# Two heads' scores in one block: the order of work in the wide attention stage is rewritten by pairs of heads

## The chip, the cores and the metric

The kernel runs on one core of one Trainium2 chip. The metric is the device time of one launch in microseconds. Three timed runs of the kernel before gave 1787.20, 1788.65 and 1789.53 us, median 1788.65 us. All float32 operands stay float32 to the outside; large products are made of three matmuls on a high part and a low rest of each operand.

## The reference, cut to what matters

The program is a sequence of transformer layers on x of 32 x 64 tokens by 256. The change lies in the first two layers, two cross-attentions to the same context with 16 heads of 128 and one learned key and value beside the 64 tokens of the context:

```python
H, K = 16, 128
qh = (q_in @ wq + bq).reshape(b, q_len, H, K)
kh = (kv_in @ wk + bk).reshape(b, t, H, K)
vh = (kv_in @ wv + bv).reshape(b, t, H, K)
kh = jnp.concatenate([kh, jnp.broadcast_to(bias_k, (b, 1, H, K))], axis=1)
vh = jnp.concatenate([vh, jnp.broadcast_to(bias_v, (b, 1, H, K))], axis=1)
logits = jnp.einsum('bqhk,bthk->bhqt', qh, kh) / scale
weights = jax.nn.softmax(logits, axis=-1)
ctx = jnp.einsum('bhqt,bthk->bqhk', weights, vh).reshape(b, q_len, H * K)
return ctx @ wo + bo
```

Ahead of each is a layer norm of x, behind it x is added back. An MLP and further layers follow and are not touched.

## The kernel before, in words

`wide_attentions` (L91 to L805) does both cross-attentions in one stream. The 2048 tokens form NG = 4 groups of 512 (GT = 4 tiles of 128). A pass takes HP = 2 heads; there are PASSES = 8 passes for each of the two attentions, so 16 passes of four groups, 64 pairs of heads and group. Within a pass the items are (group, head), ITEMS = 8 of them, and `passes` (L215) calls `slots(i, j, ...)` once for each on every engine. Each engine has its own copy of the stream in its own fixed order (POOL L341, PE L415, ACT L574, DVE L714); semaphores tie them together, and no planner is involved.

The slot of an item on TensorE (PE) has this order: turn the weights of the item before it (two transposes, L437); project its own queries (6 matmuls of 512 columns, through `product`, L81 to L83); attend for the item before it (L457, 8 instructions of 128 columns); project its keys (6 of 512); project half of the values of the pair (12 of 256); in the second head's slot, the output projection of the pair before (24 of 256, into o_ps); last its own scores (L504, 16 instructions of 65 columns on 64-column halves of the array). So the scores of one head end a slot, and the weights made from them are turned at the start of the slot after the next.

ScalarE (ACT) copies each result out of PSUM: the turned weights (L582, two halves), queries (L597), attended values (L600), the exponentials (L603), keys (L606), values (L618). VectorE (DVE) makes the softmax: maximum (L721), difference (L726), sum (L745), reciprocal (L747), weights (L749), besides the low rest of the attended values (L742) and the addition to x (L776, two heads together, which frees o_ps). GpSimd (POOL) makes low parts of the weight matrices (L322, L359), copies head biases (L317, L318) and, where a norm is due, the normalised rows (L338) and the low part of h (L348).

Some slots carry more work. TURNS turns the normalised rows of a group (8 transposes, L406) after the scores of the slot; VALUES makes the rows of the learned values (L535); the last pass of an attention (`ending_group`) adds one transpose (L441) and four products (L494) to each pair. In a slot of two heads' pair the old order puts a full slot, some 6 to 9 us, between the scores and the transposes of their weights.

## Time and profile before

| what | value |
|---|---|
| median of three runs | 1788.65 us |
| the profiled execution's own time | 1789.56 us |
| its span, first to last instruction | 1787.8 us |
| TensorE busy over the span | 1689.2 us (94%) |
| ScalarE, VectorE, GpSimd busy | 995.4, 940.1, 549.9 us |
| mean granted TensorE clock | 0.975 |
| wide stage: first and last addition to x (L776) | 48.4 and 1029.7 us |

The profiled execution lies 0.91 us above the median. Times of rows are counted from the start of its span. The wide stage takes the first 1031 us; everything behind it is the same in both kernels. "Busy" of TensorE is modelled from the starts of its instructions, so distances between starts say more than durations.

### The profile page before, as it was taken

What the parts mean: (1) busy time and instruction counts of PE and PEld (TensorE: products, weight loads), DVE (VectorE), ACT (ScalarE), POOL (GpSimd) and SP (SyncE); (2) the same over time, 40 slices, a digit from 0 to 9 for tenths busy, and PEclk for the clock granted to TensorE, in tenths of its full rate; (3) what the DMA queues carried; (4) which work ended last, traced back from release to release, by engine and by line L of the source; (5) the groups of instructions that cost most, each with busy time, mean ns of one, the idle gap of its engine ahead of it and who ended that gap; (6) DMA issues with size and microseconds to landing.
All of it is one profiled execution on the core that took longest, in us unless ns stands there. A gap on an engine that the chain in (4) does not pass through costs nothing. (4 is left out here: it accounts for less than half of the span.)

```text
span 1787.8 us, 36048 instructions
## 1 busy us (share of the span) xinstructions
PE 1689.2 (94%) x14356; PEld 1445.4 (81%) x14356; DVE 940.1 (53%) x2064; ACT 995.4 (56%) x1932; POOL 549.9 (31%) x601
## 2 busy tenths in 40 slices
PE   7999999999999999999999889899989799987699
PEld 6999999999889899999998778676766567765598
DVE  6644444444455444444444364477859656667432
ACT  4545555555545455555555355467648667776444
POOL 5301000100153010001001162257744478776311
PEclk9999999999999999999999899899989999999699
DMA  6030000000000000000000010300010000001001
GB/s 191 1 121 24 0 23 23 23 0 24 25 1 25 25 9 15 23 23 2 21 23 0 1 31 1 86 20 2 2 22 1 7 1 2 2 13 31 1 12 36
DMA packets 59135, 40.02 MB, mean 22 GB/s; under 512 B 15725, under 2 KB 58263, under 8 KB 59031
## 3 DMA queue, kind: packets, MB, share of 16 engines
q1 hardware_dynamic: 57414, 37.78, 7.4%
q8 instruction: 73, 1.20, 0.3%
q10 hardware_dynamic: 1616, 0.79, 0.2%
q14 instruction: 32, 0.25, 0.0%
HBM read 36.46 MB, written 2.10 MB: 22 GB/s over the span
## 5 line engine op out<-in xcount | busy, mean ns | idle before, releaser
L582 ACT ACTIVATE l0a_weight_t<-l0a_t_ps 64x256 f32<-64x256 f32 x256 | 97.0, 379 | 266.3 <-PE l0a_t_ps L437 256.6
L742 DVE TENSOR_TENSOR l0a_c_lo<-l0a_c_ps,l0a_c_hi 128x512 fp32r<-128x512 f32 x128 | 88.5, 692 | 236.7 <-ACT l0a_c_hi L600 236.7
L776 DVE TENSOR_TENSOR x<-l0a_o_ps,x 128x1024 f32<-128x1024 f32 x64 | 78.4, 1225 | 213.2 <-PE l0a_o_ps L83 174.8
L317 POOL COPY l0a_head_bias<-l0a_bias_cols 128x2 f32 (+1 forms) x32 | 6.3, 198 | 494.8 <-DVE l0a_logit L726 491.0
L81 PE MATMUL l0a_o_ps<-l0a_wo_hi,l0a_c_hi 128*128 128x256 f32 x512 | 149.6, 292 | 1.5 <-ACT l0a_c_hi L600 1.5
L457 PEld LDWEIGHTS l0a_c_ps<-l0a_weight_t,l0a_v 128*128 128x128 f32 x1024 | 133.9, 192 | 13.9 <-ACT l0a_weights_t L585 2.7
L82 PE MATMUL l0a_o_ps<-l0a_wo_lo,l0a_c_hi 128*128 128x256 f32 x512 | 144.6, 282 | 0.0
L83 PE MATMUL l0a_o_ps<-l0a_wo_hi,l0a_c_lo 128*128 128x256 f32 x512 | 144.6, 282 | 0.0
L81 PE MATMUL l0a_v_ps<-l0a_wv_hi,ctx_hi 128*128 128x256 f32 x512 | 144.3, 282 | 0.0
L82 PE MATMUL l0a_v_ps<-l0a_wv_lo,ctx_hi 128*128 128x256 f32 x512 | 144.2, 282 | 0.0
L83 PE MATMUL l0a_v_ps<-l0a_wv_hi,ctx_lo 128*128 128x256 f32 x512 | 142.9, 279 | 0.0
L457 PE MATMUL l0a_c_ps<-l0a_weight_t,l0a_v 128*128 128x128 f32 x1024 | 135.9, 276 | 2.0 <-ACT l0a_weights_t L585 1.1
L606 ACT ACTIVATE l0a_k<-l0a_k_ps,l0a_head_bias 128x512 f32<-128x512 f32 x128 | 88.3, 690 | 60.4 <-PE l0a_k_ps L83 60.2
L597 ACT ACTIVATE l0a_q<-l0a_q_ps,l0a_head_bias 128x512 f32<-128x512 f32 x128 | 88.1, 688 | 58.4 <-PE l0a_q_ps L83 57.6
L618 ACT ACTIVATE l0a_v<-l0a_v_ps 128x512 f32<-128x512 f32 x128 | 76.6, 598 | 76.3 <-PE l0a_v_ps L83 76.3
L81 PE MATMUL l0a_q_ps<-h_hi,l0a_w_hi 128*128 128x512 f32 x256 | 112.3, 439 | 0.7 <-POOL l0a_k L318 0.7
L81 PE MATMUL l0a_k_ps<-ctx_hi,l0a_w_hi 128*128 128x512 f32 x256 | 112.1, 438 | 0.0
L82 PE MATMUL l0a_k_ps<-ctx_lo,l0a_w_hi 128*128 128x512 f32 x256 | 101.4, 396 | 0.0
L83 PE MATMUL l0a_q_ps<-h_hi,l0a_w_lo 128*128 128x512 f32 x256 | 101.3, 396 | 0.0
L81 PEld LDWEIGHTS l0a_v_ps<-l0a_wv_hi,ctx_hi 128*128 128x128 f32 x512 | 96.2, 188 | 6.2
L82 PE MATMUL l0a_q_ps<-h_lo,l0a_w_hi 128*128 128x512 f32 x256 | 101.0, 394 | 0.0
L83 PE MATMUL l0a_k_ps<-ctx_hi,l0a_w_lo 128*128 128x512 f32 x256 | 100.7, 394 | 0.0
(435 smaller groups left out, 4883.2 us busy)
## 6 DMA issues: line engine op xcount, KB each, us to landing
l0a_raw_v<-in_L_xattn_wv_dram SPq DMA_DIRECT2D x16, 256.0 KB, 3.3
l0a_raw_o<-in_L_xattn_wo_dram SPq DMA_DIRECT2D x32, 128.0 KB, 2.8
l3a_room<-in_L_xattn_wo_dram SPq DMA_DIRECT2D x2, 2048.0 KB, 8.7
l0a_raw<-in_L_xattn_wq_dram SPq DMA_DIRECT2D x31, 128.0 KB, 2.3
l0a_raw<-in_L_xattn_wk_dram SPq DMA_DIRECT2D x31, 128.0 KB, 2.3
x<-in_x_dram SPq DMA_DIRECT2D x4, 512.0 KB, 8.0
l3a_room<-in_L_xattn_w_fc_dram SPq DMA_DIRECT2D x2, 1024.0 KB, 11.2
l3a_room<-in_ctx_dram SPq DMA_DIRECT2D x1, 2048.0 KB, 11.1
```

What stands on the lines that cost most here:

```text
L81: pe.matmul(out, wh, mh, start=start, stop=False)
L82: pe.matmul(out, wh, ml, start=False, stop=False)
L83: return pe.matmul(out, wl, mh, start=False, stop=stop)
L317: pool.tensor_copy(head_bias[p][:], bias_cols[:, BQ:BK + 1, bass.ds(h, 1)].rearrange("p a b -> p (a b)"))
L457: last = pe.matmul(by_tile[:, m, b, :, :], v[(j - HP) // HP % 2][:, m * HB + b, p * K:(p + 1) * K], weight_t[:, m, b, :, :].rearrange("p a ...
L582: last = act.activation(weight_t[half, :, :, b, :], t_ps[half, 0:GT // 2 * P] .rearrange("p (m b q) -> p m b q", b=HB, q=SEQ), ACT.Copy)
L597: act.activation(q[:], q_ps[:], ACT.Identity, bias=head_bias[p][:, 0:1]).then_inc(q_done, 1)
L606: act.activation(k[p][:, :, 0:SEQ], k_ps[:].rearrange("p (b k) -> p b k", k=SEQ), ACT.Identity, bias=head_bias[p][:, 1:2]).then_inc(k_done, 1)
L618: act.activation(v[j // HP % 2][:, p * GT // HP:(p + 1) * GT // HP, :] .rearrange("p t k -> p (t k)"), v_ps[:], ACT.Copy).then_inc(v_done, 1)
L742: dve.tensor_tensor(c[p][1][:], c_ps[:], c[p][0][:].bitcast(F32), ALU.subtract).then_inc(c_lo, 1)
L776: dve.tensor_tensor(chip.x[:, own, :], o_ps[:], chip.x[:, own, :], ALU.add).then_inc(added, 1)
```

## The change

The slot now belongs to a pair of heads and a group: `slots(i, u, ...)` with u from 1 to 4 replaces eight slots of single heads, on all engines.

On TensorE the order of a slot is: queries and keys of the first head; (rows turned, learned values, where due); the first half of the values; the four transposes of the weights of both heads of the pair before; queries of the second head; the second half of the values; attend for the first and for the second head of the pair before; keys of the second head; the output projection of the pair before; the scores of both heads of this pair, 32 instructions in one block.

The scores of the two heads lie in two PSUM banks (s_ps, 2 x 512), and the softmax is done once for both: the maximum, the difference, the exponential, the sum, the reciprocal and the weights each work on twice the elements with one instruction. To find the banks, the keys and the turned weights share one (kt_ps), and the second head's attended values are written into the queries' bank (q_ps). On ScalarE the exponential stands behind the taking of the first head's queries and ahead of its keys; the two heads' turned weights are copied in four pieces. Queries have one SBUF tile for each head. Head biases of the next pass are copied by GpSimd at the start of the next pass's first slot, behind the scores (L317, L318), and ScalarE waits for them before it takes the queries. The rows of a group are turned between the keys and the values of a slot instead of after its scores; in slot 0, ahead of the second head's keys.

```diff
-    TURNS = {0: 1, 2: 2, 4: 3, **{(PASSES - 1) * ITEMS + 6 + HP * g: NG + g for g in range(NG)}, LAST * ITEMS + 6: 2 * NG}
-    VALUES = {ITEMS: 0, (PASSES + 1) * ITEMS: 1}
-    SPREAD = {HP * HP: 0, ITEMS + 1: 1}
+    TURNS = {0: 1, 1: 2, 2: 3, **{(PASSES - 1) * NG + 3 + g: NG + g for g in range(NG)}, LAST * NG + 3: 2 * NG}
+    VALUES = {NG: 0, (PASSES + 1) * NG: 1}
+    SPREAD = {2: 0, NG: 1}
...
-        q, k = sb("q", [P, GN]), [sb(f"k{p}", [P, GT * HB, SEQ + 1]) for p in range(HP)]
+        q, k = [sb(f"q{p}", [P, GN]) for p in range(HP)], [sb(f"k{p}", [P, GT * HB, SEQ + 1]) for p in range(HP)]
         v = [sb(f"v{b}", [P, GT, HP * K]) for b in range(2)]
-        logit, expd = sb("logit", [P, GT, SEQ + 1]), sb("expd", [P, GT, SEQ + 1])
-        top, total, inverse = sb("top", [P, GT]), sb("total", [P, GT]), sb("inverse", [P, GT])
...
-        weight_t = sb("weight_t", [P, GT // 2, HB, 2, SEQ])
+        HT = HP * GT
+        logit, expd = sb("logit", [P, HT, SEQ + 1]), sb("expd", [P, HT, SEQ + 1])
+        top, total, inverse = sb("top", [P, HT]), sb("total", [P, HT]), sb("inverse", [P, HT])
...
-        q_ps, k_ps, v_ps, s_ps, t_ps, c_ps = (chip.ps(f"l0a_{x}_ps", [P, GN], stack) for x in ("q", "k", "v", "s", "t", "c"))
+        q_ps, kt_ps, v_ps, c_ps = (chip.ps(f"l0a_{x}_ps", [P, GN], stack) for x in ("q", "kt", "v", "c"))
+        s_ps = chip.ps("l0a_s_ps", [P, HP, 512], stack)
...
+        attended = (c_ps, q_ps)
...
+                def slots(i, u, this, prev, a=0):
...
+                    if this and u == NG:
+                        pool.wait_ge(s_made, n)
+                        for p in range(HP):
+                            last = head_columns((i + 1) * HP + p, p)
+                        last.then_inc(head_set, 1)
...
+                    if next_pass_in(i, u):
+                        pool.wait_ge(w_hi_done, (i + 1) * HP + 1)
+                        low_w(0).then_inc(w_split, 1)
                     if S is not None and S + 1 in TURNS:
                         normalise(TURNS[S + 1])
...
+                    if next_pass_in(i, u):
+                        pool.wait_ge(w_hi_done, (i + 1) * HP + HP)
+                        low_w(1).then_inc(w_split, 1)
...
+                    def attend(p):
+                        by_tile = attended[p][:].rearrange("p (m a b q) -> p m b a q", a=2, b=HB, q=SEQ)
+                        for m in range(GT // 2):
+                            for b in range(HB):
+                                last = pe.matmul(by_tile[:, m, b, :, :], v[(u - 1) % 2][:, m * HB + b, p * K:(p + 1) * K],
+                                                 weight_t[p][:, m, b, :, :].rearrange("p a q -> p (a q)"), start=True, stop=True)
+                        last.then_inc(c_made, 1)
...
+                        if u % NG == 0:
+                            pe.wait_ge(w_split, (i + u // NG) * HP + 1)
+                        if first_use(S) is not None and S > 0:
+                            pe.wait_ge(x_lo_done, CH * (first_use(S) + 1))
+                        project(0, 0)
+                        if S in (0, 2, 3):
+                            pe.wait_ge(ctx_lo_done, {0: 4, 2: 6, 3: 8}[S])
+                        project(1, 0)
+                    if S in TURNS and S > 0:
+                        if S == 1:
+                            pe.wait_ge(x_whole_done, CH * TURNS[S])
                         else:
                             pe.wait_ge(added, outputs_before(S))
...
+                        turn_rows(TURNS[S], half_banks)
...
+                    if this:
+                        if u % NG == 0:
+                            pe.wait_ge(wv_split, i + u // NG + 1)
+                        if prev:
+                            pe.wait_ge(v_done, heads_before(0))
+                        values(0)
...
+                    if prev:
+                        pe.wait_ge(weight_a, n)
+                        if this:
+                            pe.wait_ge(k_done, heads_before(1))
+                        for x in range(HT // 2):
+                            last = pe.transpose(kt_ps[:, x * P:(x + 1) * P], weight[:, 2 * x:2 * x + 2, :]
+                                                .rearrange("p t k -> p (t k)"), chip.ident[:])
+                        last.then_inc(t_made, 1)
+                        if ending is not None:
+                            pe.wait_ge(learned_done, n)
+                            pe.transpose(s_banks[0][:, 0:P], learned_weight[:, group_rows(ending), :]
+                                         .rearrange("p t w -> p (t w)"), chip.ident[:]).then_inc(learned_turned, 1)
...
+                        pe.wait_ge(q_done, heads_before(1))
+                        project(0, 1)
+                    if this:
+                        pe.wait_ge(v_done, heads_before(1))
+                        values(1)
+                    if S == 0:
+                        pe.wait_ge(cols_done, 1)
+                        turn_rows(TURNS[S], half_banks)
...
+                        pe.wait_ge(t_done, heads_before(-1))
+                        attend(0)
+                        pe.wait_ge(t_done, heads_before(0))
+                        if this:
+                            pe.wait_ge(q_done, heads_before(2))
+                        attend(1)
+                    if this:
+                        if S == 0:
+                            pe.wait_ge(k_done, 1)
+                        project(1, 1)
...
+                        for t in range(GT):
+                            tok = slice(t * P, (t + 1) * P)
+                            for x in range(HP):
+                                if t == 0:
+                                    pe.wait_ge(c_hi, heads_before(x - 1))
+                                    pe.wait_ge(c_lo, heads_before(x - 1))
+                                last = product(pe, o_ps[:, t, :], c[x][0][:, tok], c[x][1][:, tok],
+                                               wo[0][:, x, :], wo[1][:, x, :], start=x == 0, stop=x == HP - 1 and ending is None)
...
+                    if this:
+                        pe.wait_ge(q_done, heads_before(2))
+                        pe.wait_ge(k_done, heads_before(2))
+                        if prev:
+                            pe.wait_ge(shifted, n)
+                        for p in range(HP):
+                            for t in range(GT):
+                                for b in range(HB):
+                                    at = (t * HB + b) * SEQ
+                                    last = pe.matmul(s_ps[b * SEQ:(b + 1) * SEQ, p, t * (SEQ + 1):(t + 1) * (SEQ + 1)],
+                                                     q[p][:, at:at + SEQ], k[p][:, t // 2 * 4 + b * 2 + t % 2, :], start=True, stop=True)
+                        last.then_inc(s_made, 1)
+                    if S == 0:
+                        pe.wait_ge(ctx_lo_done, 5)
+                        turn_context(2, 1)
...
+                    if this:
+                        if u % NG == 0:
+                            act.wait_ge(head_set, i + u // NG + 1)
+                        take_queries(0)
                     if prev:
...
                         act.wait_ge(shifted, n)
                         act.activation(expd[:], logit[:], ACT.Exp, scale=SCALE).then_inc(exp_done, 1)
                     if this:
...
+                        take_keys(0)
...
+                    if this:
+                        take_values(0)
...
+                    if next_pass_in(i, u):
+                        split_w(i + 1, 0)
+                    if prev:
+                        act.wait_ge(t_made, n)
+                        for p in range(HP):
+                            for b in range(2):
+                                half = slice(b * SEQ, (b + 1) * SEQ)
+                                last = act.activation(weight_t[p][half, :, :, b, :], kt_ps[half, p * GT // 2 * P:(p + 1) * GT // 2 * P]
+                                                      .rearrange("p (m b q) -> p m b q", b=HB, q=SEQ), ACT.Copy)
+                            last.then_inc(t_done, 1)
...
                     if this:
...
+                        take_queries(1)
+                    if this:
+                        take_values(1)
+                    if S == 0:
+                        take_rows(TURNS[S], half_banks)
+                    if prev:
+                        for p in range(HP):
+                            act.wait_ge(c_made, heads_before(p - 1))
+                            act.activation(c[p][0][:], attended[p][:], ACT.Copy).then_inc(c_hi, 1)
+                    if this:
+                        take_keys(1)
+                    if next_pass_in(i, u):
+                        split_wv(i + 1)
+                        split_w(i + 1, 1)
...
+                    if prev:
...
                         dve.wait_ge(s_made, n)
...
+                        dve.tensor_reduce(top[:].rearrange("p (h t) -> p h t", h=HP), scored, AX, ALU.max).then_inc(top_done, 1)
...
+                        dve.tensor_tensor(by_head(logit[:]), scored, top[:].rearrange("p (h t a) -> p h t a", h=HP, a=1)
+                                          .to_broadcast([P, HP, GT, SEQ + 1]), ALU.subtract).then_inc(shifted, 1)
...
                         dve.wait_ge(exp_done, n)
                         dve.tensor_reduce(total[:], expd[:], AX, ALU.add).then_inc(total_done, 1)
                         dve.wait_ge(total_done, n)
                         dve.reciprocal(inverse[:], total[:]).then_inc(inverse_done, 1)
                         dve.wait_ge(inverse_done, n)
                         dve.tensor_tensor(weight[:], expd[:, :, 0:SEQ], inverse[:].rearrange("p (t a) -> p t a", a=1)
...
+                                          .to_broadcast([P, HT, SEQ]), ALU.mult).then_inc(weight_a, 1)
...
+                    if prev:
+                        for p in range(HP):
+                            dve.wait_ge(c_hi, i * (HP * NG) + HP * u + p - 1)
+                            dve.tensor_tensor(c[p][1][:], attended[p][:], c[p][0][:].bitcast(F32), ALU.subtract).then_inc(c_lo, 1)
...
+                    if prev:
+                        own = group_rows(u - 1)
```

## Rows read from the trace of the kernel before

**Rows 1.** One stretch: PE, PEld, DVE, ACT, POOL busy (count), clock, DMA share, GB/s.
```profile
200.00:300.00 100.00, 100.00 (x827) 90.37 (x826) 42.57 (x100) 52.39 (x101) 9.95 (x14) 1.00 0.07 21
```

**Rows 2.** Waits, 200 to 1100 us: who waited, for whom; total us, times, longest.
```profile
PE l0a_t_ps L437 <- DVE l0a_weight L749: 2.5, 1, 2.5
```

**Rows 3.** Timeline of TensorE, one pair of slots: start us, us, engine, line, operation, count.
```profile
303.88 0.44 PE L437 MATMUL l0a_t_ps<-ident,l0a_weight 128*128 128x128 f32 x2
...
304.39 0.39 PE L82 MATMUL l0a_q_ps<-h_lo,l0a_w_hi 128*128 128x512 f32 x1
...
305.32 0.39 PE L83 MATMUL l0a_q_ps<-h_hi,l0a_w_lo 128*128 128x512 f32 x1
305.55 1.05 PE L457 MATMUL l0a_c_ps<-l0a_weight_t,l0a_v 128*128 128x128 f32 x8
...
307.83 0.28 PE L81 MATMUL l0a_v_ps<-l0a_wv_hi,ctx_hi 128*128 128x256 f32 x1
...
309.25 0.28 PE L81 MATMUL l0a_o_ps<-l0a_wo_hi,l0a_c_hi 128*128 128x256 f32 x1
...
311.97 0.28 PE L83 MATMUL l0a_o_ps<-l0a_wo_hi,l0a_c_lo 128*128 128x256 f32 x1
312.18 0.69 PE L504 MATMUL l0a_s_ps<-l0a_k,l0a_q 128*64 128x65 f32 x16
312.80 0.44 PE L437 MATMUL l0a_t_ps<-ident,l0a_weight 128*128 128x128 f32 x2
...
318.88 0.44 PE L437 MATMUL l0a_t_ps<-ident,l0a_weight 128*128 128x128 f32 x2
```

**Rows 4.** Timeline of ScalarE in that slot.
```profile
305.75 0.69 ACT L597 ACTIVATE l0a_q<-l0a_q_ps,l0a_head_bias 128x512 f32<-128x512 f32 x1 [0.62 <-PE l0a_q_ps L83]
306.64 0.60 ACT L600 ACTIVATE l0a_c_hi<-l0a_c_ps 128x512 fp32r<-128x512 f32 x1 [0.20 <-PE l0a_c_ps L457]
307.13 0.41 ACT L603 ACTIVATE l0a_expd<-l0a_logit 128x260 f32<-128x260 f32 x1
```

**Rows 5.** Timeline of VectorE in that slot, and at the start of the next.
```profile
307.27 0.69 DVE L742 TENSOR_TENSOR l0a_c_lo<-l0a_c_ps,l0a_c_hi 128x512 fp32r<-128x512 f32 x1 [2.38 <-ACT l0a_c_hi L600]
307.88 0.41 DVE L745 TENSOR_REDUCE l0a_total<-l0a_expd 128x4 f32<-128x260 f32 x1
308.32 0.18 DVE L747 RECIPROCAL l0a_inverse<-l0a_total 128x4 f32<-128x4 f32 x1
308.54 0.42 DVE L749 TENSOR_TENSOR l0a_weight<-l0a_expd,l0a_inverse 128x256 f32<-128x256 f32 x1
...
312.29 1.22 DVE L776 TENSOR_TENSOR x<-l0a_o_ps,x 128x1024 f32<-128x1024 f32 x1 [3.25 <-PE l0a_o_ps L83]
313.43 0.42 DVE L721 TENSOR_REDUCE l0a_top<-l0a_s_ps 128x4 f32<-128x260 f32 x1
```

**Rows 6.** Groups by line and shape, 200 to 1100 us: busy us, mean ns, idle.
```profile
L504 PE MATMUL l0a_s_ps<-l0a_k,l0a_q 128*64 128x65 f32 x1680 | 72.0, 227 | 0.0
```

**Rows 7.** The same, 1100 to 1788 us, operations of other stages with 1024 elements.
```profile
L1766 DVE TENSOR_REDUCE l1a_top<-l1a_score 128x16 f32<-128x1024 f32 x32 | 38.9, 1215 | 0.6
L1713 ACT ACTIVATE l1a_score<-l1a_score 128x1024 f32<-128x1024 f32 x32 | 33.7, 1052 | 6.4 <-POOL l1a_score L1455 6.1
```

**Rows 8.** Timeline of TensorE: normalised rows turned in an ending slot.
```profile
1000.48 1.09 PE L406 MATMUL l0a_o_ps<-ident,l0a_rows 128*128 128x128 f32 x8
```

**Rows 9.** Timeline of GpSimd in the first slots.
```profile
32.40 4.85 POOL L338 TENSOR_SCALAR l0a_rows<-x,x_moments,l0a_norm_inverse 128x256 f32<-128x256 f32 x4
```

**Rows 10.** Timeline of TensorE where the wide stage runs out.
```profile
1012.12 0.44 PE L437 MATMUL l0a_t_ps<-ident,l0a_weight 128*128 128x128 f32 x2
...
1017.08 0.41 PE L437 MATMUL l0a_t_ps<-ident,l0a_weight 128*128 128x128 f32 x2 [2.51 <-DVE l0a_weight L749]
...
1018.75 2.08 PE L457 MATMUL l0a_c_ps<-l0a_weight_t,l0a_v 128*128 128x128 f32 x8 [1.15 <-ACT l0a_weights_t L585]
```

**Rows 11.** Timeline of VectorE there.
```profile
1016.51 0.42 DVE L749 TENSOR_TENSOR l0a_weight<-l0a_expd,l0a_inverse 128x256 f32<-128x256 f32 x1
```

More of the change, by code:

```diff
@@ L206, in next_head, with next_pass_in, ending_group @@
-        def next_head(i, j):
-            more = not (isinstance(i, int) and i == LAST)
-            return j - ITEMS + 1 if more and ITEMS - 1 <= j <= ITEMS else None
-        def ending_group(i, j):
-            return (j - HP) // HP if isinstance(i, int) and i in (PASSES - 1, LAST) and j % HP == HP - 1 else None
+            return S // NG // PASSES * NG + S % NG
+        def next_pass_in(i, u):
+            return u == NG - 1 and not (isinstance(i, int) and i == LAST)
+        def ending_group(i, u):
+            return u - 1 if isinstance(i, int) and i in (PASSES - 1, LAST) else None
@@ L215, in passes, with endings @@
+        def endings(i, u):
+            return i // PASSES * NG + u
         def passes(engine, slots):
-            slots(0, 0, True, False, False)
-            slots(0, 1, True, True, False)
-            for j in range(2, ITEMS + 2):
-                slots(0, j, True, True, True)
+            slots(0, 0, True, False)
+            for u in range(1, NG + 1):
+                slots(0, u, True, True)
             with engine.Fori(1, PASSES - 1) as i:
-                for j in range(2, ITEMS + 2):
-                    slots(i, j, True, True, True)
+                for u in range(1, NG + 1):
+                    slots(i, u, True, True)
@@ L233, in wide_attentions @@
+            for u in range(1, NG + 1):
+                slots(LAST, u, u < NG, True)
         with nc.Block() as block:
@@ L413, in turn_biases, with slots, heads_before, project @@
                     last.then_inc(cols_turned, 1)
-                def slots(i, j, this, mid, prev, a=0):
-                    n = i * ITEMS + j
-                    S = slot_number(i, j)
-                    p = j % HP
-                    _, cols = tiles(j)
-                    ending = ending_group(i, j)
-                    def project(x):
-                        out, made = ((q_ps, q_made), (k_ps, k_made))[x]
+                def slots(i, u, this, prev, a=0):
+                    n = i * NG + u
+                    S = slot_number(i, u)
+                    cols = group_columns(u % NG)
+                    ending = ending_group(i, u)
+                    def heads_before(more):
+                        return i * (HP * NG) + HP * u + more
+                    def project(x, p):
+                        out, made = ((q_ps, q_made), (kt_ps, k_made))[x]
                         src = ((chip.h_hi, chip.h_lo), (chip.ctx_hi, chip.ctx_lo))[x]
                         for ch in range(CH):
-                            if S == 0 and x == 0:
+                            if S == 0 and x == 0 and p == 0:
                                 pe.wait_ge(x_lo_done, ch + 1)
@@ new lines, in slots @@
+                    if prev:
+                        if S in (1, 2):
+                            pe.wait_ge(ctx_lo_done, {1: 7, 2: 8}[S])
+                        if not this:
+                            pe.wait_ge(v_done, heads_before(0))
+                        pe.wait_ge(t_done, heads_before(-1))
[4 more added lines that the diff above has]
+                        attend(1)
@@ L771, in slots @@
                         measure_group(m)
-                    if prev and p == HP - 1:
-                        own, _ = tiles(j - 2)
-                        dve.wait_ge(o_made, i * NG + (j - 1) // HP)
+                    if S in VALUES:
+                        keep_values(VALUES[S])
+                    if prev:
+                        for p in range(HP):
+                            dve.wait_ge(c_hi, i * (HP * NG) + HP * u + p - 1)
+                            dve.tensor_tensor(c[p][1][:], attended[p][:], c[p][0][:].bitcast(F32), ALU.subtract).then_inc(c_lo, 1)
+                    if next_pass_in(i, u):
+                        split_wv(i + 1)
+                    if S in SPREAD:
+                        spread_values(SPREAD[S])
+                    if S is not None and 1 <= S < 1 + NG:
+                        measure_context(S - 1)
+                    if prev:
+                        own = group_rows(u - 1)
+                        dve.wait_ge(o_made, n)
                         dve.tensor_tensor(chip.x[:, own, :], o_ps[:], chip.x[:, own, :], ALU.add).then_inc(added, 1)
```

315 lines of the change are left out of this document (107 added, 208 removed).

## The prediction

> **What bounds the kernel now.** I read the windows first. From 200 to 300 us TensorE is busy for 100.00 of 100 us at a granted clock of 1.00, with VectorE, ScalarE and GpSimd busy for 43, 52 and 10 [rows 1]. The reader is to see one full engine, so only a start that moves on TensorE moves the end. Busy time there is modelled, so I read the waits next: over 900 us TensorE waits once for the softmax weights before it turns them, 2.5 us, and that is where the stage runs out [rows 2, 10]. In the steady stretch nothing is late. Third, the timeline of a pair of slots, by distances between starts [rows 3]: 303.88 to 312.80 is 8.92 us, 312.80 to 318.88 is 6.08 us, together 15.00 us for a pair of heads and a group. There are 64 such pairs. The question is whether the new order gives TensorE less than 15.00 us of work and waiting.
>
> **TensorE's work by blocks** [rows 3]. Six products of 512 columns: (305.32 - 304.39) / 4 x 6 = 1.395 us. Turning one head's weights behind scores: 303.88 to 305.55 less the queries, 1.67 - 1.395 = 0.275. Attend for one head: 305.55 to 307.83 less the keys, 2.28 - 1.395 = 0.885. Half of the values: 309.25 - 307.83 = 1.42. Output projection, first to last start: 311.97 - 309.25 = 2.72. From the last product to the first score 0.21, where neighbours of this kind stand 0.12 apart; from the first score to the next operation 312.80 - 312.18 = 0.62. The 16 score instructions span 0.69 us with a last one of 0.23 [rows 3, 6], so 0.46 from first to last start and 0.16 from there to what follows.
>
> **What merging removes.** A score block costs about 0.09 more ahead of it and 0.13 more behind it than its own spacing, and its first steps are slow. The new slot has one block of 32 instead of two of 16. The instructions are as many as before; the second head's sixteen add about 0.48 to the first block. Transposes go from 2 + 2 to 4 in a row; one more costs (1.09 - 0.27) / 7 = 0.117, taking 0.27 as the length of one [rows 8]. So four cost 0.275 + 2 x 0.117 = 0.51.
>
> **What merging adds: the weights come later than TensorE.** Before, one full slot lay between the scores of a head and the transposes of its weights. Now only queries, keys and half of the values of the next pair do. I count from the last start of the output projection, as 0.
>
> TensorE arrives at the transposes: last score 0.21 + 0.46 + 0.48 = 1.15, queries start at 1.31, then 1.395 + 1.395 + 1.42 gives 5.52.
>
> The weights: the queries' last product starts 1.31 + 1.16 = 2.47 and ScalarE takes them 0.43 later, as 305.32 to 305.75 shows, at 2.90 [rows 3, 4]. Taking lasts 0.69, and the exponential behind it in ScalarE's order starts 0.11 before that ends (306.64 + 0.60 against 307.13): 3.48. It has 520 elements; 260 take 0.41 and 1024 take 1.052, so 0.64 / 764 a piece, 0.63 us [rows 4, 7]: 4.11. VectorE follows 0.03 later (306.64 + 0.60 against 307.27): 4.14. Sum to reciprocal is 0.44 for 260 elements; 1024 elements of a reduction take 1.215 against 0.41, 1.05 ns a piece, so 0.44 + 0.27 = 0.71: 4.85. Reciprocal to weights 0.22: 5.07. Weights 0.42 + 0.27 = 0.69, which is also what 512 elements take in L742: 5.76 [rows 5, 7]. From there to TensorE: 0.03 is the nearest hand-over between two engines, 1016.51 + 0.42 to 1017.08 is 0.15, where it had stood for 2.5 us [rows 10, 11]. I take 0.05, near the former, as the stall is short: 5.81.
>
> So TensorE stands for 0.29 us in every slot that has nothing else to do there. Does VectorE's first half bind instead? It adds to x from 0.32 to 1.54 as before, starts the maximum at 1.46 (313.43 - 311.97), the difference at 1.46 + 0.45 + 0.27 = 2.18, done 2.88: over half a microsecond before ScalarE is free of the queries. It does not. The keys' copy comes behind the exponential and ends near 5.0, before 5.81. Ends of this cost: the three doubled operations may be linear with no fixed share lost (as above), or each may cost two of the old ones: 0.19 + 0.14 + 0.15 = 0.48 more, stall 0.77. On the other side the gap behind the scores may shrink to nothing (0.16 less) and each hand-over by its 0.03: stall 0.1. I take the slopes, since 512 and 1024 elements are both seen.
>
> **The slot.** From the transposes: 0.51 + 1.395 + 1.42 + 2 x 0.885 + 1.395 + 2.72 = 9.21. Period 5.81 + 9.21 = 15.02, against 15.00. Without a stall, 5.52 + 0.47 + 8.70 = 14.69. So the merging earns 0.31 us and the late weights take it back.
>
> Is something else late? Attended values share banks with the queries: the second head's attend starts 5.81 + 0.51 + 1.395 + 1.42 + 0.885 = 10.02, the queries' copy ends near 9, behind four copies of turned weights (two take 0.77 now). Second head's low part: attend ends its starts at 10.8, copy from 11.1 to 11.7, low part to 12.4; the output projection starts at 12.30 and needs it 0.35 later. Margin 0.2, cost nothing. GpSimd's head biases are four small copies behind the scores, ahead of 2.90. The weight splits on ScalarE (0.6 each, once in four slots) fall ahead of the transposes' copies or behind the keys, with two microseconds to spare; its low parts on GpSimd need 1.5 and have three. SyncE's fetches wait for the same splits as before and have two slots. These are hidden by the 15 us of TensorE; uncovered they would cost their own 0.6 to 1.5 once in four slots.
>
> **Slots that are not ordinary.** Where rows are turned between keys and values (slots 2, 31 to 34, 63: eight transposes, 0.88 to 1.09 [rows 8]) or learned values are made (4, 36: about 7 us), this work covers the stall: 8 x -0.31 = -2.5. Slot 3 has half a cover: -0.2. Ordinary: 64 less the drain, these nine and slot 1, 53 x 0.02 = +1.1. First slots: the rows of group 2 end at 32.40 + 4.85 = 37.25 [rows 9]; I leave that time as it is. Now TensorE wants them directly behind the keys of slot 1, near 34, where the old order had a further slot of work. It goes on with the values at about 38.5 and needs 1.42 + 0.51 + 1.395 + 1.42 + 1.77 + 1.395 + 2.84 + 1.15 = 11.9: slot 2 starts at 50.4. Before, the same point was at 48.9 (first addition to x at 48.4). +1.5. The drain: 1012.12 to 1029.7, 17.6 us, in which TensorE ran at half its clock for a part: 8 attend instructions took 2.08 us against 1.05 [rows 3, 10]. Now both heads' softmax is exposed at once (weights 3.9 us behind the scores), then both attends and the projection; two waits become one. I put -1, between 0 and -4.
>
> Sum: 1.1 - 2.5 - 0.2 + 1.5 - 1.0 = -1.1 us on the profiled execution's 1789.56, which is 1788.5; that execution lay 0.91 above the median, so 1787.6.
>
> **A rule weighed.** Before the scores the trace shows 0.21 instead of 0.12, and 0.16 instead of 0.03 behind them [rows 3]. The Trainium skill, "TensorE: Matmul & The Clock Gate", section "Step-by-step: what each phase is for", says that TensorE pulls the next weight load ahead of matmuls in flight when row groups don't conflict or when the load goes to the background buffer. By that rule a change of block is free, and one block fewer saves nothing; the trace's gaps speak against it at the scores. The time this would give is rival three.
>
> **The rivals.**
> One, no stall: the weights come 0.3 earlier. For it: TensorE never waits for them now [rows 2], and four small terms of the chain are hand-overs. Against: 0.69 + 0.63 + 0.71 + 0.69 are durations, not guesses. 53 x -0.31 = -16.4, with the rest -18.6: 1770. Halfway counts as well: each 0.1 us is 5.3.
> Two, slower: the chain behind ScalarE's copy of the queries is longer, as two-head operations over two banks or broadcast patterns cost twice the old ones. Place: TensorE in front of the first transpose, in 53 slots. Price up to 0.48 x 53 = +25: 1813. It decides from 0.1 us a slot on, 1793.
> Three, block changes cost the same wherever they lie: values to transposes, values to attend and scores to queries are new neighbours. The one to the transposes hides in the stall; what is left is about 0.2 a slot: +10, 1798. For it: the gaps were seen only around scores. Against: queries to attend are 0.23 apart, no gap.
> Four, the first slots or a dropped clock in the drain cost some microseconds more: 1791 to 1795.
>
> **How the numbers follow.** Forecast 0.52, rival one 0.19, two 0.13, three 0.10, four 0.06. A difference under 0.2% (3.6 us) can't be told from none. The forecast's own range, 0.08 us a slot either way, is 1783 to 1792; it gives 0.14 faster, 0.33 same, 0.05 slower. Rival one is faster. Two is slower, three 0.06 slower and 0.04 same, four half and half. Faster 0.33, same 0.40, slower 0.27. The range of 1776 to 1799 leaves out the full rival one and the upper half of two.
>
> **What would show it.** Additions to x 15.0 us apart in the loops; the waits with TensorE before L437's successor on VectorE's weights, some 50 times 0.3 us, 15 us in all; the exponential at 0.63 and starting directly behind the queries' copy. Period 14.7 and no such wait is rival one; 15.1 and more with waits of 0.4 to 0.8 rival two; waits of 0.3 and 15.2, with gaps from values to attend, rival three. An interval of additions in slot 1 to 2 near 16 would show the first slots wrong.

## The result, and the profile after

The changed kernel takes 1797.67 us (median of 5 runs, 1796.01 to 1798.75) against 1787.65 (5 runs, 1786.93 to 1789.53): ratio 1.0053, 95% interval 1.0038 to 1.0067. It is slower by 10.0 us. The forecast was 1787.6 and no change; the time lies inside its range, but on the side that had 27 of 100, for a reason that the forecast had priced too low.

The profiled execution took 1798.05 us, its span 1796.3. First TensorE in the stretch of [rows 1]: core time, busy time of TensorE, its weight load, VectorE, ScalarE and GpSimd, granted clock, DMA share, GB/s.

```profile
200.00:300.00 100.00, 98.45 (x806) 89.06 (x807) 36.27 (x58) 51.91 (x96) 8.90 (x14) 1.00 0.07 21
```

It had been 100.00. The clock stands at its upper level (1.00, 2.4 GHz) as before, so the lost 1.55 us are waits, and the waits of 200 to 1100 us say where (who waited, for whom, total us, times, longest):

```profile
PE l0a_kt_ps L514 <- DVE l0a_weight L805: 15.7, 48, 3.9
```

Where [rows 2] showed one wait of 2.5 us, TensorE now waits 48 times. The longest, 3.9, is where the stage runs out; the other 47 share 11.8 us, 0.25 each. Before 200 us there are six more, which makes 53. L514 turns the weights of both heads, L805 makes them. Next, one slot on TensorE, VectorE and ScalarE (start us, us, engine, line, operation; in brackets the idle time before it and what ended it), to lay beside [rows 3 to 5]:

```profile
315.85 0.28 PE L83 MATMUL l0a_o_ps<-l0a_wo_hi,l0a_c_lo 128*128 128x256 f32 x1
316.05 1.15 PE L577 MATMUL l0a_s_ps<-l0a_k,l0a_q 128*64 128x65 f32 x32
317.13 0.50 PE L81 MATMUL l0a_q_ps<-h_hi,l0a_w_hi 128*128 128x512 f32 x1
317.47 0.39 PE L82 MATMUL l0a_q_ps<-h_lo,l0a_w_hi 128*128 128x512 f32 x1
...
318.40 0.39 PE L83 MATMUL l0a_q_ps<-h_hi,l0a_w_lo 128*128 128x512 f32 x1
...
321.33 0.28 PE L83 MATMUL l0a_v_ps<-l0a_wv_hi,ctx_lo 128*128 128x256 f32 x1
321.87 0.65 PE L514 MATMUL l0a_kt_ps<-ident,l0a_weight 128*128 128x128 f32 x4 [0.25 <-DVE l0a_weight L805]
322.27 0.48 PE L81 MATMUL l0a_q_ps<-h_hi,l0a_w_hi 128*128 128x512 f32 x1
322.59 0.39 PE L82 MATMUL l0a_q_ps<-h_lo,l0a_w_hi 128*128 128x512 f32 x1
```

```profile
317.30 0.69 DVE L791 TENSOR_REDUCE l0a_top<-l0a_s_ps 128x8 f32<-128x520 f32 x1
318.02 0.70 DVE L795 TENSOR_TENSOR l0a_logit<-l0a_s_ps,l0a_top 128x520 f32<-128x520 f32 x1
320.08 0.69 DVE L801 TENSOR_REDUCE l0a_total<-l0a_expd 128x8 f32<-128x520 f32 x1 [1.36 <-ACT l0a_expd L648]
320.81 0.20 DVE L803 RECIPROCAL l0a_inverse<-l0a_total 128x8 f32<-128x8 f32 x1
321.04 0.69 DVE L805 TENSOR_TENSOR l0a_weight<-l0a_expd,l0a_inverse 128x512 f32<-128x512 f32 x1
```

```profile
318.83 0.69 ACT L629 ACTIVATE l0a_q<-l0a_q_ps,l0a_head_bias 128x512 f32<-128x512 f32 x1 [4.82 <-PE l0a_q_ps L83]
319.42 0.63 ACT L648 ACTIVATE l0a_expd<-l0a_logit 128x520 f32<-128x520 f32 x1
320.23 0.69 ACT L633 ACTIVATE l0a_k<-l0a_kt_ps,l0a_head_bias 128x512 f32<-128x512 f32 x1 [0.18 <-PE l0a_kt_ps L83]
```

The reader is to see the chain. The difference is done at 318.02 + 0.70 = 318.72, but ScalarE, which works in order, first waits for the queries (318.83) and takes them for 0.69; the exponential starts at 319.42, and sum, reciprocal, weights and transposes follow without a hole. Counted from the last start of the output projection at 315.85, the transposes start at 6.02. TensorE's last product of the values starts at 321.33, so it would have been there near 321.45, at 5.60. It stands for 0.42 us; the idle time of 0.25 in brackets is less, since the end of a matmul is modelled. The period, the time from one slot to the next, is 15.23 us, against 15.00.

### The profile page after: what moved, and what is told of

It reads as the page before. It is cut to its first block and busy times, and to the rows that moved or that the text cites. A ratio compares the mean times of both kernels' runs of the same rounds, so it can differ in the third digit from the quotient of the medians.

```text
span 1796.3 us, 35533 instructions
## 1 busy us (share of the span) xinstructions
PE 1683.2 (94%) x14356; PEld 1442.2 (80%) x14356; DVE 892.6 (50%) x1680; ACT 983.1 (55%) x1868; POOL 544.5 (30%) x602
## 5 line engine op out<-in xcount | busy, mean ns | idle before, releaser
L830 DVE TENSOR_TENSOR l0a_c_lo<-l0a_c_ps,l0a_c_hi 128x512 fp32r<-128x512 f32 x64 | 44.2, 691 | 305.1 <-ACT l0a_c_hi L682 305.1
L326 POOL TENSOR_TENSOR l0a_w_lo<-l0a_raw,l0a_w_hi 128x512 fp32r<-128x512 f32 x32 | 41.8, 1307 | 464.1 <-ACT l0a_w_hi L600 464.1
L633 ACT ACTIVATE l0a_k<-l0a_kt_ps,l0a_head_bias 128x512 f32<-128x512 f32 x128 | 88.4, 690 | 62.7 <-PE l0a_kt_ps L83 62.3
L356 POOL TENSOR_TENSOR l0a_wo_lo<-l0a_raw_o,l0a_wo_hi 128x512 fp32r<-128x512 f32 x16 | 20.7, 1294 | 287.3 <-ACT l0a_wo_hi L659 287.3
L81 PE MATMUL l0a_kt_ps<-ctx_hi,l0a_w_hi 128*128 128x512 f32 x256 | 106.5, 416 | 0.0
L667 ACT ACTIVATE l0a_weight_t<-l0a_kt_ps 64x256 f32<-64x256 f32 x256 | 96.5, 377 | 13.9 <-PE l0a_kt_ps L514 10.8
L83 PE MATMUL l0a_kt_ps<-ctx_hi,l0a_w_lo 128*128 128x512 f32 x256 | 101.1, 395 | 0.0
L82 PE MATMUL l0a_kt_ps<-ctx_lo,l0a_w_hi 128*128 128x512 f32 x256 | 101.0, 394 | 0.0
L82 PEld LDWEIGHTS l0a_v_ps<-l0a_wv_lo,ctx_hi 128*128 128x128 f32 x512 | 96.6, 189 | 5.2
```

Of the source, the lines that this page charges most:

```text
L81: pe.matmul(out, wh, mh, start=start, stop=False)
L82: pe.matmul(out, wh, ml, start=False, stop=False)
L83: return pe.matmul(out, wl, mh, start=False, stop=stop)
L326: return pool.tensor_tensor(w[p][1][:], raw[p][:], w[p][0][:].bitcast(F32), ALU.subtract)
L356: pool.tensor_tensor(wo[1][:], raw_o[:], wo[0][:].bitcast(F32), ALU.subtract).then_inc(wo_split, 1)
L633: act.activation(k[p][:, :, 0:SEQ], kt_ps[:].rearrange("p (b k) -> p b k", k=SEQ), ACT.Identity, bias=head_bias[p][:, 1:2]).then_inc(k_don ...
```

## The experiments

All were timed beside the kernel before. Four ran on one chip (before 1788.82, 11 runs), three on another (before 1788.51, 7 runs).

**The exponential ahead of the queries' copy** (ScalarE alone), the test of the mechanism:

```
+   if prev: wait shifted; activation(expd <- logit, Exp)
    if this: ... take_queries(0)
-   if prev: wait shifted; activation(expd <- logit, Exp)
    if this: take_keys(0)
```

> The changed kernel with the exponential put ahead of the taking of the first head's queries on ScalarE; nothing else moves. Theory (chain): TensorE waits for the weights because the exponential stands behind the queries' copy in ScalarE's order. The difference is done 2.88 us after the last start of the output projection, so the exponential starts at 2.91 and not at 3.57, and the weights come 0.66 us earlier: 5.36 against TensorE's arrival at 5.60. No stall is left; a slot takes 14.77 us and not 15.23, 53 slots x -0.46 = -24: about 1773 us, faster than the kernel before. Rival (block changes): the added 0.23 us a slot lies in the new neighbours of the score block and of the transposes, and the wait for the weights only fills a gap that would be there anyway: 15.1 to 15.2 us, 1794 to 1798.

Measured 1775.13 us, ratio to before 0.9924 (0.9908 to 0.9939); period 14.77. ScalarE, then VectorE and TensorE, in one slot that starts with the last product at 310.24:

```profile
313.15 0.64 ACT L644 ACTIVATE l0a_expd<-l0a_logit 128x520 f32<-128x520 f32 x1 [4.75 <-DVE l0a_logit L795]
313.69 0.67 ACT L629 ACTIVATE l0a_q<-l0a_q_ps,l0a_head_bias 128x512 f32<-128x512 f32 x1
```

```profile
313.82 0.69 DVE L801 TENSOR_REDUCE l0a_total<-l0a_expd 128x8 f32<-128x520 f32 x1 [0.71 <-ACT l0a_expd L644]
...
314.79 0.69 DVE L805 TENSOR_TENSOR l0a_weight<-l0a_expd,l0a_inverse 128x512 f32<-128x512 f32 x1
```

```profile
315.72 0.28 PE L83 MATMUL l0a_v_ps<-l0a_wv_hi,ctx_lo 128*128 128x256 f32 x1
315.84 0.60 PE L514 MATMUL l0a_kt_ps<-ident,l0a_weight 128*128 128x128 f32 x4
```

The weights are done at 315.48, 0.36 before TensorE arrives, and the transposes start at 5.60 with no wait. The merged block does earn its time, and one position in ScalarE's order decides whether the kernel keeps it: -13.7 us against before here, +10.0 in the changed kernel, 23.7 between them. The slots alone give 53 x 0.46 = 24.4.

**The exponential behind the keys' copy too**, a dose the other way:

```
    take_queries(0)
+   take_keys(0)
    if prev: wait shifted; activation(expd <- logit, Exp)
-   if this: take_keys(0)
```

> The changed kernel with the exponential behind the taking of the first head's queries and of its keys. A dose of the same thing: the keys are made 4.39 us after the last start of the output projection, so the exponential starts at 4.97 and not at 3.57. Theory (chain): the whole 1.40 goes into the slot, 16.63 us, about 53 x 1.40 = +74, with the slots that turn rows +6: 1878 us. Rival (block changes): the slot hardly moves, or by less than half of it, since the wait for the weights is not what ends last.

Measured 1877.65 us (one run), period 16.63, as expected.

```profile
323.06 0.69 ACT L633 ACTIVATE l0a_k<-l0a_kt_ps,l0a_head_bias 128x512 f32<-128x512 f32 x1 [0.71 <-PE l0a_kt_ps L83]
323.64 0.63 ACT L649 ACTIVATE l0a_expd<-l0a_logit 128x520 f32<-128x520 f32 x1
```

```profile
PE l0a_kt_ps L514 <- DVE l0a_weight L804: 81.2, 52, 1.7
```

From the last start of the output projection (318.67 in this slot) the exponential starts at 4.97, against 3.57 in the changed kernel: 1.40 later, and the period is 16.63 - 15.23 = 1.40 longer. The chain has no slack at all once it is late.

**The order of two waits** ahead of the transposes. The changed kernel waits for the weights, then for the keys' bank, which has long been free. Here the late one stands last:

```
-   pe.wait_ge(weight_a, n)
    if this: pe.wait_ge(k_done, heads_before(1))
+   pe.wait_ge(weight_a, n)
    for x in range(HT // 2): (the four transposes)
```

> The changed kernel with the two waits in front of the transposes in the other order: first the one for the keys' copy, which is long done, then the one for the weights. Theory: of the 0.13 us from the end of the weights to the first transpose, 0.08 is a wait that stands as an instruction of its own and is followed by another one; with the late wait last, TensorE starts 0.05 us behind the weights, as it does at 32.4 us of the trace of before. 53 x -0.08 = -4: 15.15 us a slot, about 1793.5. Rival: 0.13 is what any restart costs behind VectorE: 15.23, 1797.7.

Measured 1794.99 us, ratio 1.0035 (1.0021 to 1.0048); period 15.17 instead of 15.23. VectorE and TensorE:

```profile
319.69 0.69 DVE L805 TENSOR_TENSOR l0a_weight<-l0a_expd,l0a_inverse 128x512 f32<-128x512 f32 x1
```

```profile
320.43 0.66 PE L514 MATMUL l0a_kt_ps<-ident,l0a_weight 128*128 128x128 f32 x4 [0.18 <-DVE l0a_weight L805]
```

From the end of the weights (320.38) to the first transpose are 0.05 us; in the changed kernel they are 0.13 to 0.14 (321.73 to 321.87). Between the two medians lie 2.7 us; 53 times 0.06 would be 3.2. The intervals of the two ratios overlap, so the total rests on the period and the rows more than on the medians.

The exchange changes the restart, but "the late wait last is the fast one" is not the rule. Of the 53 slots that stall in the changed kernel, 48 show 0.13 to 0.15, and five show 0.06 with the very same order of waits (transposes at 474.12, 491.12, 574.41, 976.85 and 993.86). VectorE and TensorE in the first of the five:

```profile
473.37 0.69 DVE L805 TENSOR_TENSOR l0a_weight<-l0a_expd,l0a_inverse 128x512 f32<-128x512 f32 x1
```

```profile
474.12 0.66 PE L514 MATMUL l0a_kt_ps<-ident,l0a_weight 128*128 128x128 f32 x4 [0.18 <-DVE l0a_weight L805]
```

With the waits exchanged the 48 show 0.05 to 0.06, and the same five 0.14 to 0.15. The place at 32.4 us of the trace of before, which the expectation takes for a late wait that stands last, is the opposite: the late wait there, for the context's low part, stands first, and TensorE starts 0.06 behind it. And in [rows 10] the late wait is the only one, and it takes 0.15. What decides between 0.05 and 0.13 stays open.

**The transposes later.** TensorE projects the second head's queries first and turns the weights behind them (L514's block moved behind `project(0, 1)`, its wait with it):

```
+   if this: ... pe.wait_ge(q_done, heads_before(1)); project(0, 1)
    if prev: (waits, four transposes of both heads' weights)
-   if this: ... pe.wait_ge(q_done, heads_before(1)); project(0, 1)
```

> The changed kernel with the four transposes of the weights put behind the queries of the second head and not in front of them; ScalarE's order as it is. Theory (chain): the weights are ready 6.02 us after the last start of the output projection, TensorE now arrives at 5.60 + 1.40 = 7.00, so nothing waits: 14.77 us a slot, about 1773 us. Next in line are the copies of the turned weights (7.8 to 9.3) ahead of the attends (at 8.9 and 9.8), hidden by 0.3. Rival (block changes): 15.1 to 15.2, 1794 to 1798. Second rival (ScalarE becomes late: queries of the second head are now taken behind the turned weights, and the second attend needs their bank): 14.9 to 15.1, waits of the attend on ScalarE.

Measured 1793.63 us, ratio 1.0028 (1.0016 to 1.004); period 15.08. The wait for the weights is gone, and another has come in its place. The waits of 200 to 1000 us, then ScalarE and TensorE:

```profile
PEld l0a_q_ps L462 <- ACT l0a_q L629: 10.5, 42, 0.3
```

```profile
322.49 1.56 ACT L667 ACTIVATE l0a_weight_t<-l0a_kt_ps 64x256 f32<-64x256 f32 x4 [0.71 <-PE l0a_kt_ps L519]
324.07 0.69 ACT L629 ACTIVATE l0a_q<-l0a_q_ps,l0a_head_bias 128x512 f32<-128x512 f32 x1
```

```profile
323.70 1.05 PE L462 MATMUL l0a_c_ps<-l0a_weight_t,l0a_v 128*128 128x128 f32 x8
324.82 1.16 PE L462 MATMUL l0a_q_ps<-l0a_weight_t,l0a_v 128*128 128x128 f32 x8
```

The second head's attend writes the bank of the queries, and ScalarE takes the queries only behind the turned weights, until 324.76. The two attends start 1.12 apart, where [rows 3] give about 0.89, and from the second to the keys are 0.91 (324.82 to 325.73), where the unstalled slot of the next experiment has 0.82: together 0.32 of the 0.33 by which the two periods differ. This was the expectation's second rival, not its theory.

**The same, and the second queries' copy ahead of the turned weights:**

```
+   if this: take_queries(1)
    if prev: (four copies of turned weights)
-   if this: take_queries(1)
    if this: take_values(1)
```

> The changed kernel with the transposes behind the second head's queries, and on ScalarE the second head's queries taken ahead of the turned weights. The kernel with the first of these two edits alone took 15.08 us a slot, with the second attend waiting for the queries' copy. Theory (chain, and ScalarE's order behind it): with the copy ahead of the turned weights it ends at 7.9 us after the last start of the output projection, the turned weights at 8.6 and 9.4, the attends come at 8.9 and 9.8: nothing waits, 14.77 us a slot, 53 x -0.46 = -24 from the changed kernel, near 1775 us as the kernel with the exponential first. Rival: a turn behind queries costs something of its own (its weight load behind a product of 512 columns), 14.9 to 15.1, 1780 to 1793.

Measured 1773.55 us, ratio 0.9909 (0.9892 to 0.9925); period 14.75. Two different orders, this one and the first, end at the same period once nothing is late. That is the unstalled slot.

**The merging alone.** With no wait left, the scores can be split again and their cost read. To the kernel just told, the first head's 16 scores are moved in front of the output projection, the second's stay behind it:

```
+   (waits) for t, b: pe.matmul(s_ps[.., 0, ..], q[0], k[0])   # before the output projection
    (output projection)
-   for p in range(HP): for t, b: pe.matmul(s_ps[.., p, ..], q[p], k[p])
+   for t, b: pe.matmul(s_ps[.., 1, ..], q[1], k[1])
```

> The kernel with the transposes later and the second head's queries first, with the score block split again: the first head's 16 score instructions stand ahead of the output projection, the second head's behind it. The number of instructions is the same. Theory: a score block costs its switches, about 0.09 ahead, 0.05 in its first step, 0.12 behind and 0.05 to 0.10 in the first step of what follows; ahead it may be hidden by a product of 512 columns. So 0.20 to 0.30 a slot more than without the split, 15.0 us against 14.77; over 63 slots +13 to +19. This is the gain of the merging, by itself. Rival (merging saves nothing, the switches are paid by whatever stands there): 14.77 either way, no difference.

Measured 1797.29 us, ratio to before 1.0044 (1.0027 to 1.0061); period 15.12, 0.37 above the same kernel with one block. TensorE with the scores split, then with one block:

```profile
312.02 0.40 PE L83 MATMUL l0a_kt_ps<-ctx_hi,l0a_w_lo 128*128 128x512 f32 x1
312.35 0.69 PE L557 MATMUL l0a_s_ps<-l0a_k,l0a_q 128*64 128x65 f32 x16
312.96 0.39 PE L81 MATMUL l0a_o_ps<-l0a_wo_hi,l0a_c_hi 128*128 128x256 f32 x1
313.19 0.28 PE L82 MATMUL l0a_o_ps<-l0a_wo_lo,l0a_c_hi 128*128 128x256 f32 x1
...
315.99 0.69 PE L588 MATMUL l0a_s_ps<-l0a_k,l0a_q 128*64 128x65 f32 x16
316.61 0.50 PE L81 MATMUL l0a_q_ps<-h_hi,l0a_w_hi 128*128 128x512 f32 x1
```

```profile
306.12 0.39 PE L83 MATMUL l0a_kt_ps<-ctx_hi,l0a_w_lo 128*128 128x512 f32 x1
306.35 0.28 PE L81 MATMUL l0a_o_ps<-l0a_wo_hi,l0a_c_hi 128*128 128x256 f32 x1
306.47 0.28 PE L82 MATMUL l0a_o_ps<-l0a_wo_lo,l0a_c_hi 128*128 128x256 f32 x1
...
309.28 1.15 PE L577 MATMUL l0a_s_ps<-l0a_k,l0a_q 128*64 128x65 f32 x32
310.36 0.50 PE L81 MATMUL l0a_q_ps<-h_hi,l0a_w_hi 128*128 128x512 f32 x1
```

A second block costs 0.10 ahead of it (0.33 instead of 0.23), 0.15 for the blocks themselves (0.61 + 0.62 from first score to what follows, against 1.08), and 0.11 in the first step of what follows (0.23 instead of 0.12): 0.36 of the 0.37. The third term is the one that the prediction did not have. The expectation had 0.20 to 0.30 a slot and +13 to +19 us; it was 0.37 and +23.7. This is the price of a second block in this place. The blocks of the old order stood elsewhere, and from the kernel before to the unstalled one the period falls by 0.25 (15.00 to 14.75), for the merging and all the other moves together.

**The first slots.** In the changed kernel TensorE waits in slot 1 for the rows that GpSimd normalises, in the middle of its products:

```profile
32.83 0.27 PE L418 MATMUL l0a_o_ps<-ident,l0a_rows 128*128 128x128 f32 x1
33.80 0.33 PE L418 MATMUL l0a_o_ps<-ident,l0a_rows 128*128 128x128 f32 x1 [0.70 <-POOL l0a_rows L342]
...
36.20 1.14 PE L418 MATMUL l0a_o_ps<-ident,l0a_rows 128*128 128x128 f32 x5 [0.87 <-POOL l0a_rows L342]
```

To the first experiment's kernel this one adds that these rows are turned behind the second half of the values, and that ScalarE takes them there:

```
-   if S in TURNS and S > 0: ... turn_rows     (behind the keys)
+   if S in TURNS and S > 1: ... turn_rows
+   if S == 1: pe.wait_ge(x_whole_done, ...); turn_rows   (behind the values' second half)
-   if S == 0: take_rows                       (ScalarE, behind take_values(1))
+   if S in (0, 1): take_rows
```

> The kernel with the exponential ahead of the queries, with the rows of group 2 turned in slot 1 behind the second half of the values, as slot 0 does, and not between keys and values; ScalarE takes them there. Theory: TensorE then does values, transposes, queries and values (4.7 us) while GpSimd makes the rows, which end at about 36.7, and of the 3.3 us that it stood in slot 1 some 0.6 is left, before the output projection, for the low part of the attended values. So about -2 us: 1773 against 1775, additions to x from 47.5 on and not from 49.7. Rival: the low part of h and the measuring behind the rows push group 3's rows back, and slot 2 gives the gain back: 1775.

Measured 1772.61 us, ratio 0.9909 (0.9893 to 0.9926), the lowest median of all. TensorE:

```profile
37.60 1.03 PE L418 MATMUL l0a_o_ps<-ident,l0a_rows 128*128 128x128 f32 x8
...
43.07 0.35 PE L81 MATMUL l0a_o_ps<-l0a_wo_hi,l0a_c_hi 128*128 128x256 f32 x1 [1.24 <-DVE l0a_c_lo L830]
```

The eight transposes run without a wait. The first addition to x comes at 46.4; in the changed kernel's profile it comes at 49.7, in the first experiment's at 50.7. A stall of 1.24 on VectorE's low part is left. It beats both kernels, but against the first experiment's kernel (0.9924) the interval does not part them; that the first slots are 3 to 4 us shorter is read from the traces.

Not all of that is the wait. While TensorE stood for the rows, its granted clock fell. From 37 to 39 us (columns as in [rows 1], the clock third from the end), the changed kernel and the kernel with the keys first:

```profile
37.00:39.00 2.00, 2.00 (x11) 2.00 (x10) 0.14 (x1) 1.72 (x3) 0.00 (x0) 0.50 0.00 0
```

```profile
37.00:39.00 2.00, 2.00 (x19) 2.00 (x18) 0.68 (x2) 1.65 (x4) 0.00 (x0) 1.00 0.00 0
```

The kernel with the keys first stands as long for the rows as the changed one, but there the clock stayed at 1.00 (it also does in this one), and the scores of slot 1 start at 47.8; in the changed kernel they start at 49.6, in the first experiment's at 50.5. So the lower level (0.50, 1.2 GHz), which the changed kernel had from 36.4 to 39.6 us and the first experiment's from 35.3 to 41.6, cost them about 1.6 and 2.7 us (the changed kernel came to the rows 0.2 later than the other two). The last slots differ in the same way: the last two additions are 16.7 us apart here and 18.2 in the first experiment's kernel, whose code is the same there but whose clock was at 0.50 for longer (about 10 us, here about 6.5). The profiled executions thus lie 6.5 us apart, the medians only 2.5.

## Why the prediction was wrong, by its own steps

**The mechanism held.** TensorE waits at the transposes, in each ordinary slot, for weights that come late because the exponential stands behind the queries' copy; the late weights take back what the merging earns. The exponential ahead of the queries, and the later transposes with the second queries ahead, remove the wait by two routes and give the 14.7 to 14.8 us of an unstalled slot. The gain "14.69" was 14.77 and 14.75. The price of the stall was too low: a period of 15.02 was forecast, 15.23 came. The 0.21 has three parts.

**"Queries start at 1.31 ... last product 1.31 + 1.16"**: start 1.28, last product 2.55. The first product behind the scores takes 0.34 to the next start (317.13 to 317.47), not 0.23. I had counted a score block's costs ahead of it and directly behind it, and the six products behind at their ordinary spacing. This puts 0.08 on the chain, and as much on the unstalled slot. The scores are not special in this: the first product behind the transposes takes 0.32 (322.27 to 322.59), and the trace of before had the same step, in the line ahead of the one that [rows 3] give for 304.39:

```profile
304.07 0.48 PE L81 MATMUL l0a_q_ps<-h_hi,l0a_w_hi 128*128 128x512 f32 x1
```

It is 0.32 there too. The reading took the spacing from 304.39 on and put the slow first step into the block ahead of it (turning, attend), so a first head's queries behind the scores got none.

**"Sum to reciprocal 0.71 ... reciprocal to weights 0.22 ... weights 5.76"**: exponential 0.63, sum 0.69, weights 0.69 were right to 0.01, and the slopes from other sizes can be trusted. Queries taken at 2.98 (2.90 forecast), exponential 3.57 (3.48), sum 4.23 (4.14), reciprocal 4.96 (4.85), weights 5.19 (5.07). The steps from sum to reciprocal and from there to weights were 0.73 and 0.23 instead of 0.71 and 0.22, and their end at 5.88 is 0.12 late: the 0.08, and 0.04 in roundings and hand-overs.

**"I take 0.05, near the former, as the stall is short: 5.81"**: 6.02. This was the term with two rows behind it, 0.03 and 0.15, and I chose by an argument (a short stall restarts fast) that no row bore. It took 0.13 to 0.14, close to the row of the same instruction pair, 0.15 [rows 10, 11]. With the two waits exchanged it takes 0.05 in the same slots, but five slots go the other way and the row had one wait only, so the cause of the size is open, and the agreement with that row may be chance. With 0.08 to 0.09 this is the largest single miss.

**"From the transposes ... 9.21"**: 9.20. So rival three's place, values to attend and values to transposes, costs nothing. Its idea was right at one boundary that it did not name so, scores to queries, by 0.10.

**The sum.** 53 slots at +0.23 instead of +0.02 are 11.1 us more. Covered slots gave -0.23 each instead of -0.31, together 0.6 less. The first slots cost +1.8 instead of +1.5 (slot 2 starts at 50.7, before 48.9). The drain took 15.7 us (last addition to x 1039.4) instead of 17.6, -1.9 where -1 stood, and what lies behind the stage was 1.1 shorter. Together 11.1 + 0.6 + 0.3 - 0.9 - 1.1 = 10.0, against 9.6 between the profiled 1798.05 and the forecast 1788.5.

Three of these terms have little to do with the new order. The +1.8 came near +1.5 by luck: the forecast had no fall of the clock in slot 1, and with the clock at 1.00 the same order on TensorE, in the kernel with the keys first, was at slot 2 at 48.9, as the kernel before. The drain is shorter because the lower level ended sooner. In the kernel before TensorE had it for some 10 us, in the changed one for about 6.5, and not in the output projection of the last pair. Before, at the lower level, and after, in that projection:

```profile
1018.00:1028.00 10.00, 7.79 (x31) 7.17 (x32) 0.69 (x1) 1.27 (x4) 0.00 (x0) 0.50 0.01 2
```

```profile
1034.00:1038.00 4.00, 3.10 (x22) 3.00 (x22) 0.69 (x1) 0.03 (x1) 0.00 (x0) 1.00 0.01 4
```

Between the last two additions lie 18.1 us before, 16.0 to 18.2 in the kernels with the new order. And the part behind the stage, the same in all, takes 756.2 to 759.0 us in the nine profiles, so 1.1 between two of them says nothing. When the clock returns in the drain differs between kernels with the same code there; why was not tried and stays open.

**The rivals.** One (no stall, 1770) is refuted for the change as made, and is what the first experiment makes of it. Two had the right place (and its sign, 15.1 and more with waits of 0.4 to 0.8: TensorE stands for 0.42, of which the profile calls 0.25 idle) and "0.1 us a slot on" as its deciding point, but its reason, doubled operations at twice the price, is refuted by the durations. Three gave nearly the right time (1798) for a reason that is mostly wrong. The rule weighed in the prediction, that a weight load is pulled ahead of matmuls in flight (the Trainium skill, "TensorE: Matmul & The Clock Gate", section "Step-by-step: what each phase is for"), does not make a change of block free here: one more block of scores costs 0.37 us.

**What the reading missed.** The forecast put 0.52 on a period within 0.08 of 15.02. With 53 slots, 0.1 us a slot decides the verdict, and the chain had nine links with some hundredths of doubt each, nearly all of one sign: most hand-overs were taken at the shortest one seen. The row nearest in kind, 0.15 for the restart, would alone have given 5.91 + 9.21 = 15.12.

## What to carry to other kernels

When a change brings a consumer nearer to its producer, follow the chain through every in-order queue that it crosses and ask which instruction stands in front of it by order only; here one exchange on ScalarE is worth 24 us of 1798. Price each hand-over and the restart of the waiting engine by the row nearest in kind, and multiply the doubt by the number of passes before choosing "no change". Before a time outside the steady slots is put down to the order of work, look at the granted clock there: in the first and last slots it moved some 1 to 3 us by itself.

## What the runs showed of the hardware

- The first 512-column product behind a block of 64-column scores takes 0.34 us to the next start instead of 0.23, behind transposes or an attend (128 columns) 0.31 to 0.32, before the change too. The first 256-column product behind scores takes 0.23 instead of 0.12 (the kernel with the scores split). One block of scores more costs 0.37 us in all there.
- TensorE's restart behind VectorE's end took either 0.05 to 0.06 or 0.13 to 0.15 us. Exchanging the late wait and a satisfied one turned 48 slots from 0.13 to 0.05 and five from 0.06 to 0.15; what decides is open.
- In slot 1 TensorE stood for 0.7 to 0.9 us three times between single transposes (33 to 36 us), and its granted clock went from 1.00 to 0.50 at about 36.5 us; with the same pauses it stayed at 1.00 in the kernel with the keys first. In the drain (before, the changed kernel, the first and the last experiment) it fell near the last transposes of weights, where TensorE mostly waits, and came back in the middle of dense work, 6.5 to 10 us later.
- From 260 to 520 elements the exponential (0.41 to 0.63 us) and the reductions (0.41 to 0.69) grew by the slopes between 260 and 1024 elements, to 0.01 us: no step from the second bank or the second head's pattern.
